# A joint query/key weight in the second attention, and the second experts' weights split during the first expert stage

## The reference, cut to what matters

```
x  = x + tanh(g_xattn[0]) * attention0(ctx, layernorm(x), mask)       # 4 heads
x  = x + tanh(g_ffn[0])   * experts0(layernorm(x))                    # 8 experts, top 2, plus a shared one
q  = layernorm(x) @ Wq + bq;  k = ctx @ Wk + bk;  v = ctx @ Wv + bv   # layer 1, one head, H = 256
x  = x + tanh(g_xattn[1]) * softmax(q @ k.T) @ v
h  = gelu(layernorm(x) @ W1[e] + b1[e])                               # e: the one expert chosen for the token
x  = x + tanh(g_ffn[1]) * score * (h @ W2[e] + b2[e])                 # W1: 8x256x512, W2: 8x512x256
```

## Time and profile before

| | |
|---|---|
| median of 3 runs | 1256.4 us (1250.9, 1256.4, 1256.54) |
| the profiled execution: its time, its span | 1255.76 us, 1253.9 us |
| busy share of the span: PE, DVE, ACT, POOL | 89%, 61%, 48%, 33% |
| mean granted PE clock | 0.94 of full speed |

### The profile page before, as it was taken

How to read it: one execution, slowest core, us unless ns; L and a number is a source line. 1 busy time by engine, 2 the same in 40 slices (tenths; PEclk the granted TensorE clock), 3 DMA queues, 4 the chain that set the end, 5 groups by cost and what they waited for, 6 DMA issues and landing times. The chain is left out here.

```text
span 1253.9 us, 31159 instructions
## 1 busy us (share of the span) xinstructions
PE 1113.0 (89%) x8451; PEld 859.0 (69%) x8452; DVE 765.0 (61%) x2494; ACT 600.4 (48%) x1400; POOL 412.0 (33%) x485
## 2 busy tenths in 40 slices
PE   3999999999999944999999999965999998289996
PEld 2677777777777733777777777744777777256664
DVE  5467777777777662344444444434788887447775
ACT  3466665666566521444444444422555555033442
POOL 3345555556465430000000000004566662212222
PEclk9799999999999866999999999986999999579999
DMA  4123121311221112222222222225764541433341
GB/s 132 32 66 101 57 69 56 101 63 55 67 82 50 45 64 71 74 79 79 79 79 79 78 79 78 79 81 156 269 192 155 165 151 59 118 89 106 109 110 52
DMA packets 94382, 116.21 MB, mean 93 GB/s; under 512 B 12479, under 2 KB 80049, under 8 KB 94066
## 3 DMA queue, kind: packets, MB, share of 16 engines
q1 hardware_dynamic: 82594, 84.50, 22.1%
q0 software_dynamic: 10576, 29.41, 6.7%
q10 hardware_dynamic: 1152, 1.58, 0.5%
HBM read 70.43 MB, written 45.92 MB: 93 GB/s over the span
## 5 line engine op out<-in xcount | busy, mean ns | idle before, releaser
L1487 DVE TENSOR_TENSOR e_z_low<-e_z_cols,e_z_high 128x256 f16<-128x256 f32 x142 | 59.9, 422 | 209.5 <-ACT e_z_high L1431 209.2
L1431 ACT ACTIVATE e_z_high<-e_z_cols 128x256 f16<-128x256 f32 x142 | 54.5, 384 | 254.8 <-PE e_z_cols L1403 254.8
L1128 PE MATMUL a_out<-a_v_ones,a_probs 128*128 128x65 f32 x1024 | 140.6, 281 | 0.0
L1128 PEld LDWEIGHTS a_out<-a_v_ones,a_probs 128*128 128x128 f32 x1024 | 126.8, 195 | 15.3 <-issue 15.3
L464 POOL DMA_INDIRECT z_rows<-r_z_tokens,r_slot_idx x96 | 96.4, 1004 | 75.8 <-ACT r_z_tokens L455 35.7
L1608 POOL IOTA a_first_numbers<- 128x2 int32 x1 | 0.1, 125 | 367.7 <-POOLq L69 367.7
L772 ACT ACTIVATE a_probs<-a_scores,a_latent_bias,a_k_scales 128x256 f32<-128x256 f32 x128 | 65.3, 561 | 94.5 <-PE a_scores L1114 57.1
L1497 DVE TENSOR_TENSOR e_hidden_low<-e_hidden_cols,e_hidden_high 128x384 f16<-128x384 f32 (+1 forms) x142 | 83.6, 588 | 36.8 <-ACT e_hidden_high L1446 36.7
L1393 PE MATMUL e_first<-w_high,e_z_high 128*128 x412 | 96.6, 316 | 4.2 <-DVE e_z_low L1487 3.5
L1393 PE MATMUL e_first<-w_low,e_z_high 128*128 x412 | 96.3, 316 | 0.0
L1393 PE MATMUL e_first<-w_high,e_z_low 128*128 x412 | 96.3, 316 | 0.0
(11 more groups left out here) (339 smaller groups left out, 3083.3 us busy)
## 6 DMA issues: line engine op xcount, KB each, us to landing
e_z_rows<-z_rows SPq DMA_DIRECT2D x142, 128.0 KB, 2.0
y_rows<-e_y_rows SPq DMA_DIRECT2D x103, 128.0 KB, 1.7
w_stage_first<-in_w SPq DMA_DIRECT2D x18, 352.0 KB
a_ctx_in<-in_ctx SPq DMA_DIRECT2D x32, 192.0 KB, 3.7
e_token_rows<-z_rows SPq DMA_DIRECT2D x39, 129.0 KB, 2.1
residual<-in_x SPq DMA_DIRECT2D x16, 256.0 KB, 3.6
z_rows<-r_z_tokens SPq DMA_DIRECT2D x16, 256.0 KB, 2.2
a_y_shared<-y_rows SPq DMA_DIRECT2D x16, 256.0 KB, 2.8
```

The lines of the kernel that those rows point to most:

```text
L1128: ins = pe.matmul(O[t][:, h * (D + 1):(h + 1) * (D + 1)], pm[x][:, jt, t * P:(t + 1) * P], va[p][:, jt, h, :], start=i + x == 0, stop=i + ...
L1431: act.activation(xh[p][:].rearrange("p k s -> p (k s)"), ZT[:, 0:KC * P], ACT.Copy).then_inc(zhigh, 1)
L1487: v.tensor_tensor(xl[p][:].rearrange("p k s -> p (k s)"), ZT[:, 0:KC * P], xh[p][:].rearrange("p k s -> p (k s)"), ALU.subtract).then_inc( ...
```

## The change

- Attention of layer 1: the product of the transposed query weight and the key weight (with the key bias as column 193) is made once, before the first batch (`join_weights` on PE: four products of 193 columns and four of one column; `joint_weights` copies them on ACT). The query projection then has 193 output columns and carries the key weight and both biases; the scores are taken against the context columns themselves, whose row 193 is one. The key projection, its copy with bias on ACT and the tiles `k_cols` are gone. The context columns get a second buffer; `score` now reads them in two chunks of 128 and 65 rows.
- The 16 steps of `Weights` (layer 1) leave the attention: its loads on SP, `high` on ACT and `low` on DVE. `Weights` serves layer 0 alone.
- A class `NextWeights` does that work in the first expert stage: 64 pieces of 128x256, one in each of the steps 12 to 75 (loads three steps ahead, four staging tiles), at the end of SP's, ACT's and DVE's step. `over_tiles` therefore writes out steps -3 to 11, loops over 12 to 71, writes out 72 to 75, loops over 76 to 99 without the pieces, and writes out the rest, for every engine of that stage.
- The layer-1 weights stand in SBUF beside the layer-0 weights (allocated from the right side), one expert's chunks after another, W1 with 16 columns of padding.

```
+class NextWeights:
+    FIRST, PIECES, AHEAD = 12, 8 * E, 3
...
+    def load(self, sp, i, q):
+        if not isinstance(i, int) or i >= 4:
+            sp.wait_ge(self.low_done, i - 2)
...
+        sp.dma_start(self.stage[q][:], rows).then_inc(self.landed[q], 16)
+
+    def high(self, act, i, q):
...
+        act.wait_ge(self.landed[q], (i - q) * 4 + 16)
+        act.sem_inc(self.g["carried_a"], 1)
+        act.activation(high[:, ds(at, C)], self.stage[q][:], ACT.Copy, scale=WSCALE).then_inc(self.high_done, 1)
+
+    def low(self, v, i, q):
...
+        v.wait_ge(self.high_done, i + 1)
+        v.scalar_tensor_tensor(low[:, ds(at, C)], self.stage[q][:], WSCALE, high[:, ds(at, C)], ALU.mult, ALU.subtract).then_inc(self.low_done, 1)
...
 # over_tiles
+    if next_weights:
+        first, end = next_weights.FIRST, next_weights.FIRST + next_weights.PIECES
+        loops = [(first, end - 4, True), (end, end + (n - 3 - end) // 4 * 4, False)]
+    else:
+        loops = [(8, 8 + (n - 3 - 8) // 4 * 4, False)]
...
 # phase_experts, layer 0: at the end of a step of SP, of ACT, of DVE
+                    if next_piece(s, AHEAD, filling):
+                        next_weights.load(sp, s - FIRST + AHEAD, (q + AHEAD) % 4)
...
+                    if next_piece(s, 0, filling):
+                        next_weights.high(act, s - FIRST, q)
...
+                    if next_piece(s, 0, filling):
+                        next_weights.low(v, s - FIRST, q)
...
 # phase_attn1, SP, ACT, DVE
-                    if within(n + 3, weights.parts):
-                        weights.load(sp, n + 3, 1 - q)
...
-                        bias_q_or_k(n + 1, 1 - q, 1)
-                    if not early and within(n + 1, weights.parts):
-                        weights.high(act, n + 1, 1 - q)
...
-                    if within(n + 1, weights.parts):
-                        weights.low(v, n + 1, 1 - q)
...
 # phase_attn1, PE
+                def join_weights():
+                    for k in range(KC):
+                        for h in range(KC):
+                            ins = pe.matmul(WB[:, k * (DC + 1):(k + 1) * (DC + 1)], wq[:, h, k * P:(k + 1) * P], wk[:, h, :], start=h == 0, stop=h == KC - 1)
+                    ins.then_inc(joined, 1)
...
-                    pe.wait_ge(freed_act, count(2 * m))
-                    for i in range(KC):
-                        for k, (o, w) in enumerate(CTX_CHUNKS):
-                            ins = pe.matmul(PJ[1][:, i * S:(i + 1) * S], wk[0:w, k, i * P:(i + 1) * P], cT[0:w, k, :], start=k == 0, stop=k == 1)
...
-                        for k in range(KC):
-                            ins = pe.matmul(SC[:, t * S:(t + 1) * S], qT[p][:, k, t * P:(t + 1) * P], kT[p][:, k, :], start=k == 0, stop=k == KC - 1)
+                        for k, (o, w) in enumerate(D_CHUNKS):
+                            ins = pe.matmul(SC[:, t * S:(t + 1) * S], qT[p][0:w, k, t * P:(t + 1) * P], cT[p][0:w, k, :], start=k == 0, stop=k == KC - 1)
...
+                    if isinstance(n, int) and n == -1:
+                        join_weights()
```

More of the change, by code:

```diff
@@ L109, in program @@
         g["padding"] = sb("padding_rows", [P, W1])
-        with ExitStack() as l0:
+        with ExitStack() as l1, ExitStack() as l0:
+            right = lambda name, shape, dt: l1.enter_context(nc.sbuf_tensor(name, shape, dt, side="right"))
             g["w13h"] = sb("w13_high", [P, KC * (E + 1) * 2 * F0], F16, l0)
@@ L180, with __init__ @@
 class Weights:
[L186 to L199, removed]
+    def __init__(self, nc, g, a, c):
+        self.g, self.parts, self.F, self.EW = g, 2 * (E + 1), 2 * F0, E + 1
+        self.first_rows = a["w13"].rearrange("e c f -> (e c) f")
+        self.second_rows = a["w2"].rearrange("e f c -> (e f) c")
+        self.high1, self.low1, self.high2, self.low2 = (g[x][:] for x in ("w13h", "w13l", "w2h", "w2l"))
+        self.stage1 = [c.enter_context(nc.sbuf_tensor(f"w0_stage_first{p}", [P, self.F], F32)) for p in range(2)]
+        self.stage2 = [c.enter_context(nc.sbuf_tensor(f"w0_stage_second{p}", [P, 2 * C], F32)) for p in range(2)]
+        sem = lambda n: phase_semaphore(nc, g, f"w0_{n}")
         self.landed = [sem(f"landed{p}") for p in range(2)]
         self.high_done, self.low_done = sem("high_done"), sem("low_done")
[L203 to L206, removed]
+        self.second = [[(0, P, 0, 0)], [(P, P, 1, 0), (2 * P, F0 - 2 * P, 2, 1)]]
     def pieces(self, j, q):
@@ L220, in load @@
             sp.dma_start(self.stage2[q][0:rows, place * C:(place + 1) * C],
[L221 removed]
+                         self.second_rows[ds((j - q) * (F0 // 2) + row, rows), :]).then_inc(self.landed[q], 16)
     def high(self, act, j, q):
@@ L1271, in ahead, with over_tiles, run @@
             self.of(1)
-def over_tiles(eng, step, n, experts=None):
-    def run(s, q):
+def over_tiles(eng, step, n, experts=None, next_weights=None):
+    def run(s, q, filling):
         if experts:
             experts.s, experts.q = s, q
[L1280 to L1292, removed]
+        step(s, q, filling)
+    if next_weights:
+        first, end = next_weights.FIRST, next_weights.FIRST + next_weights.PIECES
+        loops = [(first, end - 4, True), (end, end + (n - 3 - end) // 4 * 4, False)]
+    else:
+        loops = [(8, 8 + (n - 3 - 8) // 4 * 4, False)]
+    at = -3
+    for first, end, filling in loops:
+        for s in range(at, first):
+            run(s, s % 4, True)
+        if experts:
+            experts.enter_loop(first)
+        with eng.Fori(first, end - 3, 4) as s:
+            for q in range(4):
+                run(s + q, q, filling)
+        if experts:
+            experts.leave_loop()
+        at = end
+    for s in range(at, n + 3):
+        run(s, s % 4, True)
 def phase_experts(nc, a, g, layer, out=None):
@@ L1337, in phase_experts, with next_piece @@
         biased, y_biased, slot_step = sem("biased"), sem("y_biased"), sem("slot_step")
+        next_weights = NextWeights(nc, g, a, c) if layer == 0 else None
+        FIRST, AHEAD = NextWeights.FIRST, NextWeights.AHEAD
+        def next_piece(s, ahead, filling):
+            return layer == 0 and filling and within(s - FIRST + ahead, NextWeights.PIECES)
         slf, sel, less = sb("slots", [P, NT * 2]), sb("slot_after", [P, NT * 2, E]), sb("slot_less", [P, NT * 2])
@@ L1705, in _ @@
             def _(v):
-                v.memset(cT[ONES:ONES + 1, 1, :], 1.0).then_inc(ones_ready, 1)
+                for x in cT:
+                    v.memset(x[ONES:ONES + 1, 1, :], 1.0).then_inc(ones_ready, 1)
                 chains = {}
```

145 lines of the change are left out of this document (89 added, 56 removed).

## The result

The change made the kernel faster: 1241.33 us (median of 8 runs) against 1254.01 us (8 runs), a ratio of 0.9914 (95% interval 0.9889 to 0.9938), which is 10.8 us of 1254. In other runs of both on a second chip the ratio was 0.9945 (0.9919 to 0.9970), or 6.9 us. The forecast was 8.9 us less, 1247 us. The profiled execution took 1240.48 us, its span was 1238.7 us.

A forecast was written before the change was run, and what follows sets the result against it. It took PE to bound the first expert stage and a PE-DVE ring of 12.22 us the attention of layer 1. Terms -4.7 - 3.7 - 3 + 2.5 = -8.9 us gave 1247 us; range 1235 to 1260, the forecast's own 1241 to 1252.

The forecast's parts named there:

- The ring: Attention of layer 1: the path PE's turn, logits, DVE's choice, normalized rows, with handovers, sets the step at 12.22 us.
- the dear end of that term: Attention steps: scores in chunks of 128 and 65 rows might cost 0.5 us a step, 6 us dearer over twelve.
- The end of the attention: Last two steps, PE-bound: without key products and the wait for biased keys, 3.7 us less; ends 2 and 5.
- The first expert stage: 64 added pieces covered by PE; the new loop shape costs 2.5 us more; ends 1.8 and 3.1.
- The start: First attention steps: POOL starts about 2 us earlier, departed loads give 1 us; together 3 us less, ends 0 and 6.
- Rival (d), the clock: Attention: PE idles 2.1 us a step and TensorE's clock falls, half of twelve steps hit: 1269 us; chance 0.15.
- signs of being wrong: Attention steps of 10 to 11 us, expert steps over 3.4 us, or a granted clock under 1.00 in the steady part.
- (a): Attention: PE is the bound and every key product counts, 39 us less there, time 1219 us; chance 0.04.
- (b): Attention: the ring closes faster, DVE or POOL bounds steps at 11.3 to 12.0 us, time 1236 to 1244; chance 0.13.
- (c): First expert stage: the pieces are not covered, 9.6 us return, time 1256.5, no change; chance 0.20.
- (steady): Twelve steady attention steps: each loses the 0.39 us slack between ring and step, 4.7 us less in all.

The follow-up runs named there:

- the second profile: Profile of the changed kernel, unaltered, run again on a second chip: 1244.44 us, ratio 0.9945 to the kernel before.
- joint_alone: Kernel before plus the joint weight only; layer-1 weight loads and halves stay in the attention: 1256.82 us, ratio 1.0040 to the kernel before.
- weights_alone: Kernel before with only the layer-1 weights moved to the first expert stage, separate key projection kept: 1252.51 us, ratio 1.0012 to the kernel before.
- ring_cut: Changed kernel, but PE makes scores and logits before turning the next rows, ACT exponentials before column copies: 1256.87 us, ratio 1.0046 to the kernel before.

## Why the prediction was right, step by step

- **The ring.** Right. 12.22 us was worked out, and the step shown above took 12.18 by the same path; PE waits 1.42 + 0.67 = 2.1 us in it, as foretold. DVE's new wait, 0.61 us, stands one operation earlier than foretold, before the maxima and not before the copy of the logits. The scores in chunks of 128 and 65 rows took 1.90 us where they had 1.89, so the dear end of that term did not come. With the ring cut and the clock held the step fell to 11.95 us, with no work taken from DVE. That the mean of 12.21 meets 12.22 is luck: it mixes written-out steps of 11.8 to 11.9, looped ones of 12.2 to 12.3 and three of 12.5 to 12.7; the second profile has 12.47, and 12.16 is what the steps take with the clock held.
- **Neither removal alone.** The two halves gave +0.40% and +0.12% (the second within its noise) and together -0.86% or -0.55%. With its clock kept the joint weight alone is bound by DVE at 12.65 us, the moved weights alone by PE at 12.47: in the kernel before the two engines were level, and only taking from both lets the step fall to the ring.
- **The end of the attention.** Right: 3.35 us to the last scores and 0.33 from there to the maxima (1048.48 - 1046.19 = 2.29), 3.7 in all, 3.7 predicted.
- **The first expert stage.** Right: looped steps are 3.32 us in both loops, pieces and all. From the first products of tile 7, where the clock has risen in every profile, to those of tile 102 it took 317.3 to 317.4 us in the three profiles of the old loop shape and 319.4 to 319.6 in the eleven of the new one. That is 2.1 to 2.3 us more; 2.5 were predicted. The two entries show as 525.31 - 521.13 = 4.18 and 739.58 - 735.50 = 4.08 us. The 0.2 us more between the two profiled executions of before and after hides this, for the first few tiles ran 2.1 us longer in that of before.
- **The start: the term that was mis-sized.** 3 us predicted, 0.8 measured (0.33 to the first turn, 0.50 from there to turn 3). The prediction put 2 us on POOL's start, which hangs on the output of batch 0. POOL begins its work on that batch's variances at 883.66 in the kernel before and at 880.87 after (POOL's timelines):

```profile
883.66 0.55 POOL L318 TENSOR_TENSOR r_rstd<-r_mean_var,eps_tile 128x2 f32<-128x2 f32 x1 [4.68 <-DVE r_mean_var L332]
```

```profile
880.87 0.19 POOL L353 TENSOR_TENSOR r_rstd<-r_mean_var,eps_tile 128x2 f32<-128x2 f32 x1 [4.05 <-DVE r_mean_var L367]
```

  From the first turn that is 25.72 us before and 26.00 after: nothing came of the 2 us. Two things took them. The step from turn 0 to turn 1 got only 0.76 us shorter (12.54, now 11.78). Before, PE's projections of batch 0 set it, for the next turn waited for ACT's copy of the value products (PE's timeline before):

```profile
870.48 0.63 PE L1851 MATMUL a_turn<-ident,a_x_norm 128*128 128x128 f32 x4 [0.84 <-ACT a_v_tokens L1664]
```

  After, POOL's chain for batch 1 sets it, four gathers and the power, 865.70 - 859.69 = 6.0 us. That chain starts 4.8 us after the first turn in both kernels. POOL's timeline after:

```profile
859.69 1.03 POOL L1573 DMA_INDIRECT a_y_chosen<-y_rows,a_slots  x1 [5.77 <-DVE a_slots L1797]
...
864.98 0.72 POOL L1678 TENSOR_TENSOR a_rstd<-a_rstd,minus_half 128x2 f32<-128x2 f32 x1
```

  And the next step lost the clock: behind a wait of 1.88 us PE ran the scores of batch 0 in 3.03 us, where 1.90 is full clock, and the step took 11.77 us (10.72 before).

```profile
866.65 0.83 PE L1921 MATMUL a_turn<-ident,a_x_norm 128*128 128x128 f32 x4 [1.88 <-DVE a_x_norm L1832]
...
868.12 3.03 PE L1948 MATMUL a_scores<-a_ctx_cols,a_q_cols 128*128 128x256 f32 x8
```

  joint_alone kept the clock there, with a longer wait (2.57 us): that step took 10.10 us, POOL began on the variances 24.33 us after the first turn, and the start to turn 3 took 33.63 us (35.48 before, 34.98 after). So some 1.4 us of the 2 exist, and in the changed kernel the clock took them. The 1 us put on the loads that left came nearly whole: from that point to the power for batch 3's rows POOL takes 7.27 us, 8.05 before, and 7.28 in weights_alone, which drops the same loads.
- **Rival (d), the clock.** The mechanism was real and given too little weight (0.15), and one of the prediction's own signs of being wrong, a clock under 1.00 inside the steady part, came (0.93 to 0.98). By the profiles it cost the changed kernel 0.7 to 3.8 us of its steady part, not 22. Between the turns of batches 3 and 15 it hit the output products behind the wait in one step of the first profile, in four of the second and in six of joint_alone's, and added 1.1 to 1.7 us to those that it hit (3.01 to 3.62 us for 1.89). In joint_alone and ring_cut it ate the whole gain. The Trainium skill, page "TensorE: Matmul & The Clock Gate", section "A second HAM failure mode: psum-queue depth-cycling", says that short idle times between groups of products make the clock swing between its levels and cost throughput. The traces agree in part: 0.60 and 0.54 stood behind a wait of 1.61 us in joint_alone, but in the first profile of the changed kernel one wait of 1.67 us lost the clock and two others of 1.67 us left the products behind them at 1.89 us.
- **Rivals (a) to (c).** No step of 10 us (a) came; (b), a ring that closes sooner, is refuted by DVE's wait for the scores and the step of 12.18 us; (c), uncovered pieces, by 3.32 us.

The sum of 8.9 us lies between the two measured gains of 10.8 and 6.9, and that is in part luck. Its four terms, the expert stage taken like against like, measure -4.8 (steady), -3.7 (end), -0.8 (start) and +2.2 (expert stage), or -7.1 us in the first profile; in the second the steady part gave only 1.7. Stretches in which the sum has nothing, from the last maxima on, were 3.2 us shorter in the first pair of profiles (1.2 and 2.0); no run here tells how much of that the change made, for they differ by as much between profiles of kernels that are alike there. The clock, which differed from run to run in the stages' first steps and behind the short waits, keeps the time from being told more closely.

## What to carry to other kernels

Where two engines are both nearly full, follow the path that joins them through one step and back: its length is what the step fell to here when both were relieved, and relieving one alone bought nothing. Before you take work from PE, look at what it will wait for: behind waits of 1.6 us a step the clock fell often enough here to make a kernel with less work slower, and a few idle products inside that wait, no longer than it, gave this back. Reordering against the ring paid only with the clock held.

## What the runs showed of the hardware that was not expected

- The same wait ahead of the same products cost the clock in one step and not in the one before it (1.65 us ahead of 1.99 and of 3.65 us in ring_cut). At the stage's start a wait of 2.57 us kept the clock in joint_alone and one of 1.88 us lost it in the kernel after. What decides is not shown here. Taking key products of 2.40 us a step from PE in joint_alone made its steady part 6.5 us longer.
- A product in f32 of 256 columns is two instructions of some 0.22 us each: five idle products took 2.2 us.
- The first expert product of layer 0, with nothing changed ahead of it, came between 476.1 and 490.5 us from profile to profile. What moves it is not shown.
